# A two-layer hypergraph block on one core: the opening of the first two batches reordered

## What is computed

```python
def hypergraph_conv(x, adj, W, b):
    H = (adj != 0).astype(x.dtype)
    w = adj.reshape(N, -1)[:, :C]                    # adj's first row weighs the hyperedges
    xw = jnp.einsum('ncd,hd->nch', x, W)
    Dn = jnp.einsum('nce,ne->nc', H, w)              # node degrees, then inverted where > 0
    Be = H.sum(axis=1)                               # edge counts, then inverted where > 0
    m = Be[:, :, None] * jnp.einsum('nce,nch->neh', H, xw)
    return Dn[:, :, None] * jnp.einsum('nce,neh->nch', H, m) + b

h = jnp.maximum(_layernorm(x), 0.0)                  # h0
z = jax.nn.relu(hypergraph_conv(h, adj, W1, b1))     # 256 -> 512
z = layer_norm(z, gamma, beta)
y = hypergraph_conv(z, adj, W2, b2)                  # 512 -> 256
out = x + (y + h)
```

## Time and profile before

| | |
|---|---|
| median of three runs | 662.37 us |
| the profiled execution | 663.38 us |
| its span, first to last instruction | 661.6 us |
| TensorE busy | 623.1 us, 94% of the span, 4744 matmuls |
| weight loads busy | 467.4 us, 71% |
| VectorE busy | 490.3 us, 74% |
| ScalarE busy | 290.9 us, 44% |
| POOL busy | 114.0 us, 17% |
| mean granted TensorE clock | 0.990 of full speed |

### The profile page before, as it was taken

The page is one execution under the profiler, slowest core; times in us unless marked ns, Lnnn a source line. Parts: engine busy times, 40 slices in busy tenths (PEclk is TensorE's granted clock), DMA queues, the critical chain, the costliest instruction groups (busy, mean ns, idle before and its releaser), DMA issues.

```text
span 661.6 us, 11883 instructions
## 1 busy us (share of the span) xinstructions
PE 623.1 (94%) x4744; PEld 467.4 (71%) x4744; DVE 490.3 (74%) x1145; ACT 290.9 (44%) x539; POOL 114.0 (17%) x137
## 2 busy tenths in 40 slices
PE   0997579999999999999999999999999999999998
PEld 0743465768858687668867688577876688586887
DVE  6879968788668966799478877599577994478632
ACT  3243483636344553536425363536435354224720
POOL 5317110401221030400303021300304012000000
PEclk9999689999999999999999999999999999999999
DMA  8992539013991079511990159700994029200801
GB/s 319 207 362 57 96 73 334 41 33 96 197 345 33 1 173 248 217 33 36 219 347 38 33 134 187 316 33 1 198 267 172 33 68 211 41 1 2 191 2 63
DMA packets 146214, 90.29 MB, mean 136 GB/s; under 512 B 134768, under 2 KB 135408, under 8 KB 141168
## 3 DMA queue, kind: packets, MB, share of 16 engines
q1 hardware_dynamic: 146160, 89.54, 49.5%
HBM read 47.58 MB, written 8.39 MB: 85 GB/s over the span
## 4 chain that ended last, share of the span: by engine, by line
PE 86%; DVE 9%; ACT 3%; DMA 1%; issue 0%; DVEq 0%; ACTq 0%
PE acc L544 17%; PE acc L561 17%; PE acc L488 15%; PE acc L525 12%; PE acc L505 11%; PE acc L468 6%; PE acc L470 6%; DVE incidence L830 1%; PE acc L420 1%; PE acc L422 1%; DVE z L892 1%; ACT z_split_ring L631 1%; ACT z L632 1%; DVE junk L839 1%; DVE stat L897 1%; DVE h_split L821 1%
## 5 line engine op out<-in xcount | busy, mean ns | idle before, releaser
L544 PE MATMUL acc<-xw_split,incidence 128*128 128x256 f16 x1024 | 113.2, 273 | 0.0
L561 PE MATMUL acc<-edge_means,incidence_t 128*128 128x256 f16 x1024 | 113.1, 273 | 0.0
L592 ACT ACTIVATE edge_means<-acc,edge_inverse 128x256 f16<-128x256 f32 x128 | 55.9, 474 | 124.4 <-PE acc L544 69.7
L468 PE MATMUL acc<-h_split,incidence 128*128 128x257 f16 x448 | 100.6, 276 | 10.1 <-DVE incidence L830 10.1
L544 PEld LDWEIGHTS acc<-xw_split,incidence 128*128 128x128 bf16 x1024 | 100.1, 98 | 13.2 <-DVE xw_split L928 0.2
L561 PEld LDWEIGHTS acc<-edge_means,incidence_t 128*128 128x128 bf16 x1024 | 100.2, 98 | 13.1
L470 PE MATMUL acc<-h_split,incidence 128*128 128x256 f16 x448 | 100.6, 276 | 0.0
L488 PE MATMUL acc<-incidence_t,edge_means 128*128 128x512 bf16 x448 | 97.8, 379 | 0.0
L525 PE MATMUL acc<-w_split,z 128*128 128x256 f16 x768 | 87.4, 275 | 5.4 <-POOL w_split L400 4.1
L525 PEld LDWEIGHTS acc<-w_split,z 128*128 128x128 f16 x768 | 75.4, 99 | 16.4 <-POOL w_split L400 4.3
L505 PE MATMUL acc<-w_split,pt_split 128*128 128x512 f16 x384 | 84.2, 379 | 2.5 <-POOL w_split L395 2.5
(11 more groups left out here) (93 smaller groups left out, 625.5 us busy)
## 6 DMA issues: line engine op xcount, KB each, us to landing
adj_in<-adj SPq DMA_DIRECT2D x32, 1024.0 KB, 10.9
out<-residual SPq DMA_DIRECT2D x32, 256.0 KB, 2.5
x_in<-x SPq DMA_DIRECT2D x7, 1024.0 KB, 5.7
edge_weights<-adj SPq DMA_DIRECT2D x8, 512.0 KB, 3.7
x_in<-x SPq DMA_DIRECT2D x2, 512.0 KB, 4.5
incidence_t<-incidence SPq DMA_TRANSPOSE x32, 4.9
z<-w1t SPq DMA_DIRECT2D x1, 512.0 KB, 4.8
xw_split<-w2t SPq DMA_DIRECT2D x1, 512.0 KB, 10.2
```

The source lines that it names most:

```text
L468: nc.tensor.matmul(acc[:, 0:ONE + 1], inc[:, b.slot, ct, cols], h0[:, ct, 0:ONE + 1], start=(ct == 0), stop=False)
L544: last = nc.tensor.matmul(acc[:, 0:DOUT], inc[:, b.slot, ct, P * et:P * (et + 1)], xw[:, ct, part, :], start=(ct == 0 and part == HI), sto ...
L561: last = nc.tensor.matmul(acc[:, 0:DOUT], inc_t[:, b.slot, ct, et, :], edge[:, et, part, :], start=(et == 0 and part == HI), stop=(et == T ...
L592: return nc.scalar.activation(o, i, ACT.Copy, **kw)
```

## The change

The steady part keeps its instructions; PSUM places move by four banks for every stage from the first D on. In the opening:

- h0 of batch 0 goes to the upper half of `z` (`u_first`), whole, instead of the ring `u`; ScalarE no longer waits for POOL to read the ring in batch 0.
- POOL waits until all eight incidence tiles and all h0 tiles of batch 0 are made; it then adds x and h0, makes one maximum over the partitions for both weights at once, adds b2, and makes W1's low half. In batch 1 it adds h0, makes W2's low half, and then adds b2.
- The degrees of batch 0 are 64 small matmuls of `inc_t` with the first row of adj, which is passed in once more as columns (`first_weights`, the same values in another shape), split into three bf16 parts by `split_weights`. The eight passes of `degree` for batch 0 go, and the load of `edge_w` for it.
- `bias_times_w2` and `first_degrees` stand inside B0, between its halves.
- W1, W2, gamma and beta are loaded right after adj of batch 0. x of batch 1 is loaded between the second and third transpose.
- VectorE runs the weights' maxima and `factor(0)` ahead of the first `edge_inverse`; the incidence of batch 1 is made mostly ahead of the drains of C0; statistics and normalisation of z go in two halves.

The diff, cut to its core (lines of "..." stand for what is left out):

```diff
-    BIAS_BANK = (2 * T + 4) % 8
+    BIAS_BANK, DEGREE_BANK = 7, 6
+    WPARTS = 3
...
+        u_first = z[:, T // 2:T, :].rearrange("p a (k d) -> p (a k) d", d=DIN)
...
-                at = (0, 3 * T)[k] if opening else 8 * T + 4 + PER_BATCH * (k - 2)
+                at = (0, 2 * T + 4)[k] if opening else 8 * T + PER_BATCH * (k - 2)
...
             def load_x(b):
-                wait_reuse(sp, res_ready, b.count(T, 0))
+                if b.offset == 1:
+                    sp.wait_ge(x_added, T)
+                else:
+                    wait_reuse(sp, res_ready, b.count(T, 0))
...
+            for q in range(QUARTERS):
+                load_adj(b0, q)
+            sp.dma_start(gb[:, 1, :], beta).then_inc(weights_loaded, 16)
+            sp.dma_start(gb[:, 0, :], gamma).then_inc(weights_loaded, 16)
+            sp.dma_start(w_col[:, 0, :], first_weights).then_inc(col_loaded, 16)
+            sp.dma_start(w1f, w1t.rearrange("(t p) h -> p t h", p=P)).then_inc(w1_loaded, 16)
+            sp.dma_start(w2f, w2t.rearrange("(t p) o -> p t o", p=P)).then_inc(w2_loaded, 16)
             sp.dma_start(b2_row[:, :], b2.to_broadcast([P, DOUT])).then_inc(b2_loaded, 16)
...
+                transpose_inc(b0, q)
+            load_x(nxt)
             for q in range(2, QUARTERS):
                 sp.wait_ge(inc_ready, QT * (q + 1))
...
+            b0, nxt = Batch(0, 0), Batch(0, 1)
+            pool.wait_ge(inc_ready, T)
+            pool.wait_ge(u_ready, T)
+            for t in range(T):
+                nc.gpsimd.tensor_tensor(res[:, 0, t, :], x_in[:, t, :], u_tile(b0, t), ALU.add).then_inc(x_added, 1)
             pool.wait_ge(max_here, 1)
-            nc.gpsimd.partition_all_reduce(wall[:, 0:1], wm[:, 0:1], P, RMAX).then_inc(max_all, 1)
+            nc.gpsimd.partition_all_reduce(wall[:, 0:2], wm[:, 0:2], P, RMAX).then_inc(max_all, 1)
+            pool.wait_ge(x_added, T)
+            pool.wait_ge(b2_loaded, 16)
+            for t in range(T):
+                nc.gpsimd.tensor_tensor(res[:, 0, t, :], res[:, 0, t, :], b2_row[:, :], ALU.add).then_inc(res_ready, 1)
             pool.wait_ge(w_hi, 1)
             nc.gpsimd.tensor_tensor(w1s[:, :, LO, :], w1f, w1s[:, :, HI, :], ALU.subtract).then_inc(w_ready, 1)
-            first_residual(Batch(0, 1))
-            pool.wait_ge(max_here, 2)
-            nc.gpsimd.partition_all_reduce(wall[:, 1:2], wm[:, 1:2], P, RMAX).then_inc(max_all, 1)
+            add_h0(nxt)
             pool.wait_ge(w_hi, 2)
             nc.gpsimd.tensor_tensor(w2s[:, :, LO, :], gf, w2s[:, :, HI, :], ALU.subtract).then_inc(w_ready, 1)
+            add_b2(nxt)
...
+            def first_degrees():
+                pe.wait_ge(col_step, 5)
+                for ct in range(T):
+                    for et in range(T):
+                        last = nc.tensor.matmul(acc_ring[:, DEGREE_BANK, WPARTS * ct:WPARTS * (ct + 1)],
+                                                inc_t[:, 0, ct, et, :], w_part[:, et, :],
+                                                start=(et == 0), stop=(et == T - 1))
+                last.then_inc(first_degree, 1)
...
             def first_stage_b():
                 for half in range(2):
+                    if half == 1:
+                        bias_times_w2()
                     for q in (2 * half, 2 * half + 1):
                         pe.wait_ge(inc_t_ready[q], 16)
+                    if half == 1:
+                        first_degrees()
...
             def stage_a(b):
                     if opening:
-                        pe.wait_ge(c_drained, min(et + 5, T))
-                        if et == 4:
-                            pe.wait_ge(bias_read, 1)
+                        pe.wait_ge(c_drained, et + 1)
...
         # ScalarE, after the high halves of h0 of batch 0
+            for ht in range(HT_):
+                last = copy(gf[:, ht, :], w2f[:, ht, :], scale=gb[:, 0, ht:ht + 1])
+            last.then_inc(gamma_w2, 1)
+            for et in range(T):
+                t1_hi_part(b0, et)
+            act.wait_ge(w1_scale, 5)
+            copy(w1s[:, :, HI, :], w1f, scale=wr[:, 2:3])
+            copy(w1f, w1f, scale=wr[:, 2:3]).then_inc(w_hi, 1)
+            root_x(b1_)
+            drain_b(b0, 0)
+            drain_b(b0, 1)
+            for g in range(GROUPS):
+                h0_tiles(b1_, g)
+                h0_hi_part(b1_, g)
             act.wait_ge(w2_scale, 5)
             copy(w2s[:, :, HI, :], gf, scale=wr[:, 3:4])
             copy(gf, gf, scale=wr[:, 3:4]).then_inc(w_hi, 1)
+            drain_b(b0, 2)
+            drain_b(b0, 3)
...
         # VectorE, after the last incidence tile of batch 0
-            for ct in range(4):
-                degree(b0, ct)
+            split_weights()
...
+            dve.wait_ge(w1_loaded, 16)
+            largest(0, w1f)
+            dve.wait_ge(gamma_w2, 1)
+            largest(1, gf).then_inc(max_here, 1)
+            factor(0, w1_scale, 1.0 / (H0_SCALE * PT_SCALE * W_SCALE))
             for half in range(2):
                 edge_inverse(b0, half)
                 for et in range(T // 2 * half, T // 2 * (half + 1)):
                     t1_lo_part(b0, et)
...
+            drain_c(b0, 0)
+            drain_c(b0, 1)
+            z_stats(b0, 0)
+            drain_c(b0, 2)
+            incidence(nxt, 3)
+            drain_c(b0, 3)
...
```

More of the change, by code:

```diff
@@ L52, in wait_reuse, with hypergraph_block @@
         eng.wait_ge(sem, value)
-def hypergraph_block(nc, x, adj, w1t, b1, gamma, beta, w2t, b2, out):
+def hypergraph_block(nc, x, adj, first_weights, w1t, b1, gamma, beta, w2t, b2, out):
     N, C, DIN = x.shape
@@ L265, in load_edge_weights @@
             def load_edge_weights(b):
[L267 removed]
+                if b.offset > 1:
+                    sp.wait_ge(deg_done, b.count(T, 0))
                 if isinstance(b.loop, int):
@@ L360, in _, with add_h0 @@
             nc.gpsimd.memset(h0[:, :, ONE:ONE + 1], 1.0).then_inc(ones_set, 1)
-            def first_residual(b):
-                pool.wait_ge(b2_loaded, 16)
-                pool.wait_ge(x_loaded, b.count(16, 16))
-                for t in range(T):
-                    nc.gpsimd.tensor_tensor(res[:, b.slot, t, :], x_in[:, t, :], b2_row[:, :],
-                                            ALU.add).then_inc(res_base, 1)
-                pool.wait_ge(res_base, b.count(T, T))
+            def add_h0(b):
@@ L1094, in _ @@
             second_degree_factor(b0)
-            for t in range(T):
-                if t % (T // 2) == 0:
-                    edge_inverse(nxt, t // (T // 2))
-                if t >= 2:
-                    z_lo(b0, t)
-                t1_lo_part(nxt, t)
+            incidence(nxt, 2)
+            h0_lo(nxt, 3)
+            b_lo(b0, 2)
+            b_lo(b0, 3)
+            dve.wait_ge(rows_loaded, 16)
+            dve.wait_ge(dn_step, N_STEPS)
+            dve.wait_ge(x_added, T)
+            drain_c(b0, 0)
[4 more added lines that the diff above has]
+            drain_c(b0, 3)
+            z_stats(b0, 1)
+            drain_c(b0, 4)
+            z_stats(b0, 2)
+            z_stats(b0, 3)
+            drain_c(b0, 5)
+            variance(z_ln, z_stat, z_half, b0, Z_STEPS, DH, lower)
+            drain_c(b0, 6)
+            z_stats(b0, 4)
+            inverse_root(z_ln, z_half, b0, Z_STEPS, ZN_SCALE, lower)
+            drain_c(b0, 7)
+            z_stats(b0, 5)
+            z_stats(b0, 6)
+            z_stats(b0, 7)
+            variance(z_ln, z_stat, z_step, b0, Z_STEPS, DH, upper)
+            z_lo(b0, 0)
+            z_lo(b0, 1)
+            inverse_root(z_ln, z_step, b0, Z_STEPS, ZN_SCALE, upper)
+            z_lo(b0, 2)
+            z_lo(b0, 3)
+            edge_inverse(nxt, 0)
+            t1_lo_part(nxt, 0)
+            for t in range(T // 2, T):
+                et = t - T // 2 + 1
+                z_lo(b0, t)
+                if et == T // 2:
+                    edge_inverse(nxt, 1)
+                t1_lo_part(nxt, et)
+            for et in range(T // 2 + 1, T):
+                t1_lo_part(nxt, et)
             for n in range(N - 2):
@@ L1128 @@
         "adj": np.ascontiguousarray(adj),
+        "first_weights": np.ascontiguousarray(np.transpose(np.reshape(np.asarray(adj)[0, 0, :], (-1, P)))),
         "w1t": np.ascontiguousarray(np.transpose(L0_gnn_W1)),
```

243 lines of the change are left out of this document (111 added, 132 removed).

## The result

| | before | after |
|---|---|---|
| median | 662.49 us, 6 runs (661.37 to 662.81) | 658.15 us, 6 runs (655.35 to 659.70) |
| profiled execution, its span | 663.38, 661.6 | 658.91, 657.1 |
| end of D0 in the span | 107.66 | 101.56 |
| from there to the span's end | 553.9 | 555.5 |

The change is faster: 0.9937 of the time before, 95% interval 0.992 to 0.9954. That is 4.3 us where 10.9 had been forecast.

What follows compares the result with a forecast made beforehand. TensorE has no waits after 107.66 us, so only the opening could gain. C0 at 60.0 plus 36.8 ends D0 at 96.8, 10.9 us earlier; counted from 662.37 this gives 651.5 us, range 642.0 to 658.5.

Steps and rivals of the forecast that it cites:

- B0's lost clock: At B0's start, TensorE's clock is lowered after idling from 28.6 to 38.4 us, costing about 2.2 us.
- added for the h0 ring: Between C0's start and D0's end, POOL's late adds hold the h0 ring and ScalarE's drain of B0: 0.7 us.
- Steps 1 and 2: Opening: A0 starts near 11.6 us instead of 17.1; B0, behind POOL's maximum, starts at 38.4 instead of 34.4.
- The quiet start: Before A0, POOL stays off until incidence is made, so VectorE runs faster; last incidence ends 6.1 us earlier.
- rival (b): Start: VectorE's 0.65 us steps come from loads, not POOL, so everything is 6.1 us later: 657.6 us; chance 0.06.
- rival (c): VectorE's in-order wait for the maximum makes it slower; decides at a POOL price of 18.8 us; chance 0.03.
- rival (a): POOL's change of work costs nothing on the way in; B0 starts at 30.5, time 642.9 us; chance 0.20.
- the term for w1's low part: Ahead of C0, POOL changes back, adds b2 and subtracts, delivering it at 52 to 53 us, wanted at 60.
- Step 3: B0 with bias product (1.9 us) and degrees (3.5) inside: C0 starts at 60.0 us against 50.9, 9.1 later.
- Step 4: C0's start to D0's end takes 36.8 us instead of 56.8, a gain of 20.0, with A1 following without wait.
- step 1: Start, POOL kept off: small VectorE operations and incidence pairs shorten; A0 ends near 28.6 us, 5.6 us earlier.
- the prediction's signs of being wrong: B0 near 30 us, A0 near 17, degree matmuls far off 3.5, a wait between C0 and A1, TensorE waits behind D0.

Runs made afterwards that it cites:

- experiment 4: Kernel after with POOL's partition maximum replaced by a TensorE product with a matrix of ones, scale taken from that sum: 649.93 us, 0.98 of before.
- 1: Kernel after with POOL's sixteen adds of b2 (batches 0 and 1) held until C0's last product: 658.78 us, 0.9953 of before.
- 2: Kernel after with VectorE's edge means put ahead of the weight factor, POOL's order untouched: 655.23 us, 0.9897 of before.
- 3: Kernel after with batch 0's eight adds of b2 moved behind w2's low part on POOL: 656.14 us, 0.9907 of before.
- 5: Kernel after with the TensorE sum in place of POOL's maximum and the edge means ahead of the weight factor: 648.19 us, 0.9779 of before.
- 6: Kernel after with B0's second result ahead of batch 1's last h0 group and incidence tiles 4 and 5 on VectorE and ScalarE: 656.46 us, 0.9909 of before.
- 7: Kernel after with TensorE sum, edge means first, and B0's second result earlier, all together: 647.71 us, 0.9773 of before.
- 8: Kernel 7 with POOL's w2 low part held for six tiles of C0 and batch 1's b2 adds until z's last normalised tile: 644.49 us, 0.9725 of before.
- 9: Kernel after, maximum kept on POOL, with edge means first and batch 0's b2 adds behind w2's low part: 652.46 us, 0.9846 of before.
- 10: Kernel 9 with B0's second result also earlier in VectorE's and ScalarE's order: 652.0 us, 0.9843 of before.
- 11: Kernel after with z of batch 0 normalised over all eight tiles at once, as before the change: 660.26 us, 0.9963 of before.

## Why the prediction was wrong

| step | predicted | measured |
|---|---|---|
| last incidence of batch 0; A0 from, to | 19.8; 11.6, 28.6 | 19.77; 11.67, 27.4 |
| POOL's eight adds end | 26.5 | 25.42 |
| change of code, way in | 7.9 | 8.64 |
| maximum ends | 35.6 | 34.43 |
| B0 starts | 38.4 | 37.09 |
| B0's lost clock; bias; degrees | 2.2; 1.9; 3.5 | 2.5; 1.89; 1.75 |
| C0 starts | 60.0 | 56.73 |
| C0's start to VectorE's first drain | 1.8 | 11.03 |
| first drain to first split of z | 12.8 | 12.24 |
| first split of z to D0's end | 21.5 | 21.56 |
| added for the h0 ring | 0.7 | no part shown |
| C0's start to D0's end | 36.8 | 44.8 |
| D0 ends | 96.8 | 101.56 |
| from there to the span's end | 553.9 | 555.5 |

**Steps 1 and 2 held.** The quiet start was had (small steps 0.16 us), so rival (b) is out, and rival (c) with it: POOL's price is at most 8.64 us and not 18.8. POOL had been free since 25.42 us; for the first 1.65 us of its pause VectorE's maxima were not ready (27.07), for the other 6.99 nothing that the profile shows held it. Whether the price counts from the last add or from the maxima is not shown; rival (a) falls either way, and experiment 4 shows the price from the other side. The Trainium skill (GPSIMD Engine Reference, Instruction dispatch) gives about 6 us for loading the code of a POOL kernel at its first call. The trace agrees that there is such a price without an instruction of its own; its sizes, 6.99 to 8.64 and 10.82 us here, 7.20 and 8.67 before, are larger, and it came at each change. In the term for w1's low part, 7.9, 5.5 to 7 and 2.1 us make 15.5 to 17 and not 16 to 17; nothing hung on it.

**Step 3 was too dear by 2.0 us.** The degrees took 1.75 us, 27 ns for each pair of a weight load and a matmul of three columns, where I had made 53 ns from the two clocks of a load. A load still showed 95 to 98 ns; one started every 27 ns, so the loads overlapped, and the part of a load that grows with the lowered clock didn't set the pace. The estimate of 107 ns a load that I had drawn from the Trainium skill (TensorE: Matmul & The Clock Gate, LDWEIGHTS) lies further off still; the trace decides. B0's lost clock was right: its first half took 9.56 us for 7.07.

**Step 4** was right that POOL's wait for w2's low part would vanish, that A1 would follow C0 without a wait, and in its chain from the first drain on. **It failed at the start of that chain**, "The first drain is 1.8 us after C0's start": it came 11.03 us after, because the preparation, which stands ahead of the drains in VectorE's order, lasted until 66.56 us. The first drain, and ScalarE's first split of z:

```profile
67.76 1.39 DVE L923 SCALAR_TENSOR_TENSOR z<-acc,dn_conv,b_row 128x512 f32<-128x512 f32 x2
```

```profile
80.00 0.80 ACT L663 ACTIVATE z_split_ring<-z,z_ln 128x512 f16<-128x512 f32 x1
```

I had written that the incidence of batch 1 "is done ahead of C0 or in its first 6 us"; the last of its tiles that stand ahead of the drains was done 8.8 us after C0's start. The time at which POOL would be busy I had nearly right (from 43.5 us, measured 45.25). What I left out is what I had used myself in step 1: POOL's adds stretch VectorE. There I counted it as a gain when they leave VectorE's path; in step 4 they arrive on it, and I charged only ScalarE's ring, 0.7 us. ScalarE did wait 4.99 us for the ring, but VectorE had work all that time. At the lengths that they have with POOL quiet, VectorE's operations in the preparation come to about 8 us, an estimate: three pairs of tiles at 1.2 us from start to start, four low halves at 0.6, the small steps about 2. They took 16.41 us, so about 8 of the 9.2 us are POOL's stretch, and the rest is VectorE's queue itself.

That D0's end hangs on this chain and not on TensorE's own waits shows in all the kernels:

| kernel | first drain | first split of z | D0 ends | last two apart |
|---|---|---|---|---|
| after | 67.76 | 80.00 | 101.56 | 21.56 |
| 1 | 63.40 | 80.55 | 102.11 | 21.56 |
| 2 | 62.49 | 75.31 | 97.10 | 21.79 |
| 3 | 63.20 | 77.39 | 98.95 | 21.56 |
| 4 | 58.31 | 71.09 | 92.66 | 21.57 |
| 5 | 56.76 | 69.53 | 91.10 | 21.57 |
| 6 | 66.74 | 80.02 | 101.59 | 21.57 |
| 7 | 55.75 | 69.02 | 90.58 | 21.56 |
| 8 | 53.85 | 66.24 | 87.90 | 21.66 |
| 9 | 57.17 | 73.47 | 95.13 | 21.66 |
| 10 | 56.19 | 72.40 | 94.03 | 21.63 |
| 11 | 67.96 | 82.56 | 104.04 | 21.48 |

The wait in C0 (5.82 us) and the lowered clock behind it (7.80 - 5.34 = 2.46 us) come from the same late preparation. Their sum is near the 8.0 us by which step 4 missed, but that is chance: between 7 and 8 TensorE saved 5.9 us in A1's wait and clock, and D0 ended 2.7 us sooner, as the first split of z came 2.8 us sooner.

The Trainium skill (SBUF — State Buffer, "SBUF: two separate sides") says why two such engines could meet: VectorE and GpSimd share one pair of ports, and whoever starts first holds it for the whole instruction; on VectorE's side that goes for operations in a two-port mode or with two inputs from SBUF beside a POOL instruction that reads SBUF. The trace agrees where an add takes 0.69 us and a VectorE step of 0.16 us beside it takes 0.65, and where the step at 61.63 us lasted as long as POOL's subtraction; that a lock is the cause, no run here shows.

**The tail** was 1.6 us longer than before: 1.5 us of it is the last batch's wait for z's last transpose (the fourth wait in the first fence). A wait behind D0 was among the prediction's signs of being wrong, as were degrees far off 3.5 us. After and the eleven kernels have 554.1 to 555.9 us there; the longest such wait was 0.2 and 0.4 us in the two in which D0 ended after 102 us (11 and 1) and 1.4 us or more in the others. What sets it was not tested and stays open.

So 10.9 us forecast, plus 3.3 (B0 and C0 earlier), less 8.0 (step 4), less 1.6 (tail), is 4.6 us; the two profiled executions differ by 4.5.

What was **shown** by experiments: less of POOL beside VectorE, with VectorE's work unchanged, makes the preparation shorter and D0 earlier (7 to 8), if the work moved finds a place where VectorE has time (8, not 1). Without the maximum on POOL, its way in and its way out together, the kernel is 8.2 us faster than after (4). The place of B0's second low half doesn't win much back (6, 10). What is only **argued**: how VectorE and POOL hinder each other inside, and how much of the 8.2 us is the way in and how much the way out. What is **untested**: the drains of C0 ahead of batch 1's incidence.

## What to carry to other kernels

When a change moves work of one engine in time, charge what it does to the engine beside it at the place where it lands, and not only at the place it leaves; a rate read from windows (us of stretch per us of overlap) gives a first estimate, though it differs with the operations that meet. A maximum over the partitions between elementwise work on POOL cost a pause both ways here: put nothing in order behind it that doesn't need it, or let another engine do it. Find the chain that sets a stage's end before adding up the waits of its engine: here D0's end followed the first split of z to 0.3 us, whatever TensorE had waited. When a wait is taken away by another order, look one stage on for the same wait before counting it as gained.

## What the runs showed that I had not expected

- 64 pairs of a weight load and a matmul of three columns ran in 1.75 us. Each load showed 95 to 98 ns, as in B0 (98 ns mean), so the loads overlapped.
- POOL's pause varied: on the way out 10.63 to 12.29 us in the kernels that kept the maximum, on the way in 8.38 to 8.95 from the last add, or 6.1 to 7.3 from the time at which VectorE's maxima were ready. The times of some of them scatter: 655.35 to 659.70 us in after and 654.15 to 657.89 in experiment 2, against 647.58 to 648.04 in 7; but 3, with the maximum, has 655.69 to 656.68, and 4, without it, 647.96 to 650.23. What makes the scatter was not tested.
- A wait of TensorE cost it more than its length where the clock was lowered behind it: 2.3 us more in A1 of experiment 6 after 4.27 us idle, 2.7 us in C0 of experiment 2 after 7.59 us, 1.7 us in C0 of experiment 3 after 2.33 us; nothing in C0 of experiment 1 after 1.36 us, and nothing in C0 of the kernel before after 2.48 us. By the table above, such a loss in C0 or A1 did not move D0's end.
